# A gated cross-attention block with its slot order turned round: which projection follows the scores

## What the kernel computes

```
x      (8, 256, 128)   queries; ctx (8, 512, 128) keys and values; 16 heads of 64
xn     = layernorm(layernorm(x)) ;  q = xn @ w_q ;  k, v = split(ctx @ w_kv)
scores = einsum('bqhd,bkhd->bhqk', q * 64**-0.5, k) ;  attn = softmax(scores)
x      = x + tanh(g_xattn) * (attn @ v @ w_out + b_out) * tanh(gate)
tokens = layernorm(x) ; expert = argmax(softmax(tokens @ gate_w)), 8 experts, 160 places each
x      = x + tanh(g_ffn) * prob * (relu(token @ w1[expert]) @ w2[expert])
```

## Time and profile before

| | |
|---|---|
| device time, median of 3 runs | 523.41 us (522.75 to 524.91) |
| the profiled execution, its own time | 525.39 us |
| its span | 523.4 us |
| PE, DVE, ACT, POOL busy in the span | 82%, 74%, 65%, 70% |
| granted TensorE clock, mean over the span | 0.948 of full speed |
| DMA queue of SyncE, share of 16 engines | 82.9% |

### The profile page before, as it was taken

How to read it: one execution, slowest core, us unless ns; L and a number is a source line. 1 busy time by engine, 2 the same in 40 slices (tenths; PEclk the granted TensorE clock), 3 DMA queues, 4 the chain that set the end, 5 groups by cost and what they waited for, 6 DMA issues and landing times.

```text
span 523.4 us, 12954 instructions
## 1 busy us (share of the span) xinstructions
PE 430.0 (82%) x5084; PEld 347.4 (66%) x5084; DVE 389.0 (74%) x825; ACT 340.5 (65%) x548; POOL 365.2 (70%) x272
## 2 busy tenths in 40 slices
PE   5777886798899889988999889988988899663393
PEld 3455665677678767866777767776867687463393
DVE  4777888478997899888988898889888888703022
ACT  4575887267777877687768777777687767700140
POOL 2774768377797779777978697869876877741115
PEclk9797999699999999999999999999999999968598
DMA  7799999969999898989897989798979798970301
GB/s 220 220 168 174 176 207 232 201 123 173 182 155 189 148 173 177 171 148 173 178 190 139 163 176 203 120 183 157 183 138 173 154 175 142 182 123 11 102 11 40
DMA packets 285772, 83.13 MB, mean 159 GB/s; under 512 B 268404, under 2 KB 283172, under 8 KB 285713
## 3 DMA queue, kind: packets, MB, share of 16 engines
q1 hardware_dynamic: 284336, 79.01, 82.9%
q0 software_dynamic: 1376, 3.30, 1.8%
HBM read 10.83 MB, written 5.14 MB: 31 GB/s over the span
## 4 chain that ended last, share of the span: by engine, by line
PE 28%; POOL 21%; DVE 16%; issue 16%; ACT 11%; DMA 6%; SPq 1%; POOLq 0%; ACTq 0%; DVEq 0%
POOL PARTS L560 16%; DVE MXL L768 7%; ACT P L638 6%; PE psEF L963 5%; PE psX L1130 5%; DMA PT<-PARTS 4%; PE psAB L1038 3%; DVE HL L755 3%; PE psEF L965 3%; PE psEF L964 3%; DVE VL L761 2%; PE psCD L1038 2%; PE psEF L1229 1%; ACT VH L611 1%; ACT PARTS L648 1%
## 5 line engine op out<-in xcount | busy, mean ns | idle before, releaser
L560 POOL TENSOR_TENSOR PARTS<-P,PARTS 128x1024 f16<-128x1024 f32 x128 | 271.8, 2142 | 92.1 <-DVE PARTS L779 74.9
L1060 PE MATMUL psO<-VH,PT 128*128 128x65 f16 x1024 | 102.4, 195 | 15.8 <-DMA PT<-PARTS 15.8
L606 ACT ACTIVATE HL<-psEF 128x768 fp32r<-128x768 f32 x63 | 51.1, 812 | 85.7 <-PE psEF L965 85.7
L1060 PEld LDWEIGHTS psO<-VH,PT 128*128 128x128 f16 x1024 | 93.9, 98 | 18.3 <-DMA PT<-PARTS 10.8
L1061 PE MATMUL psO<-VL,PT 128*128 128x64 f16 x1024 | 102.4, 194 | 0.0
L1062 PE MATMUL psO<-VH,PT 128*128 128x65 f16 x1024 | 102.2, 195 | 0.0
L1061 PEld LDWEIGHTS psO<-VL,PT 128*128 128x128 f16 x1024 | 94.0, 99 | 0.6
L1062 PEld LDWEIGHTS psO<-VH,PT 128*128 128x128 f16 x1024 | 94.2, 98 | 0.0
L638 ACT ACTIVATE P<-psAB,NB 128x512 f32<-128x512 f32 x128 | 80.7, 687 | 5.5 <-DVE NB L771 5.5
L638 ACT ACTIVATE P<-psCD,NB 128x512 f32<-128x512 f32 x128 | 81.7, 701 | 0.2
L768 DVE TENSOR_REDUCE MXL<-psAB 128x2 f32<-128x1024 f32 x64 | 77.8, 1215 | 1.1 <-PE psAB L1038 1.1
(11 more groups left out here) (177 smaller groups left out, 762.3 us busy)
## 6 DMA issues: line engine op xcount, KB each, us to landing
ctx_raw<-in_ctx_dram SPq DMA_DIRECT2D x8, 256.0 KB, 3.7
w1s<-in_L_ffn_w_dram SPq DMA_DIRECT2D x8, 256.0 KB, 3.5
PT<-PARTS SPq DMA_TRANSPOSE x128, 4.7
w2s<-in_L_ffn_w_dram SPq DMA_DIRECT2D x8, 256.0 KB, 4.6
experts_table<-zeros POOLq DMA_DIRECT2D x2, 645.0 KB, 4.2
PARTS<-experts_table SPq DMA_DIRECT2D x2, 516.0 KB, 4.3
wraw<-in_L_xattn_w_kv_dram SPq DMA_DIRECT2D x4, 256.0 KB, 5.0
out_dram<-row SPq DMA_DIRECT2D x8, 128.0 KB, 2.8
```

The costliest lines, as they stand in the source:

```text
L560: pool.tensor_tensor(PARTS[:, par, qt, 1], P32[:, par, qt], PARTS[:, par, qt, 0], ALU.subtract).then_inc(plo_done, 1)
L606: act.activation(HL[:, hp % 2, H_KHI:H_KHI + KQ], kq_bank(j)[:, 0:KQ], ACT.Copy).then_inc(kq_hi_done, 1)
L1060: pe.matmul(psO[:, g:g + DH + 1], phi, VH[:, kt, head, 0:DH + 1], start=first_, stop=False)
```

## The change

The order of each engine's calls in a slot is turned round. No instruction is added or removed, and none changes its shape.

- TensorE: `v_project` (and `x_transposes`, `logits`) come directly behind the scores, then `values`, then `k_project` and `q_project`, then the transposes and `project`. The bank of V now has to be free of pair j+1, not of pair j+2.
- VectorE: `kq_lo` moves from behind the second maximum to the head of the next slot; `v_lo` (and `choose`) stand between the first and the second maximum. In slot hp = 3 `phi_first` and the normalising come ahead of `add_attention`.
- ScalarE: `v_hi` and `xt_hi` come ahead of the exponentials, `kq_hi` behind them; then `phi_second`, and the copies `ot_copy`, `ctxt_hi`, `tokt_copy` last.

```diff
 # ScalarE, batch(b)
                 for j, hp in slots(b):
+                    if v_group(b, hp):
+                        v_hi(*v_group(b, hp))
+                    if hp == X_STEP and not is_last(b):
+                        xt_hi(b + 1)
+                    exps(b, hp, 0)
+                    exps(b, hp, 1)
                     if not (is_last(b) and hp + AHEAD >= PAIRS):
                         kq_hi(*next_pair(b, hp, AHEAD))
-                    exps(b, hp, 0)
-                    exps(b, hp, 1)
+                    phi_second(b, hp)
                     if ot_group(b, hp):
                         ot_copy(*ot_group(b, hp))
                     if hp == CTX_STEP and not is_last(b):
                         ctxt_hi(b + 1)
...
-                    if v_group(b, hp):
-                        v_hi(*v_group(b, hp))
-                    phi_second(b, hp)
-                    if hp == X_STEP and not is_last(b):
-                        xt_hi(b + 1)
 # VectorE, batch(b)
                 for j, hp in slots(b):
+                    if j and not (is_last(b) and hp + AHEAD > PAIRS):
+                        kq_lo(*next_pair(b, hp, AHEAD - 1))
                     row_max(b, hp, 0)
+                    if v_group(b, hp):
+                        v_lo(*v_group(b, hp))
+                    if hp == LOGITS_STEP and not is_first(b):
+                        choose(b - 1)
                     row_max(b, hp, 1)
-                    if not (is_last(b) and hp + AHEAD >= PAIRS):
-                        kq_lo(*next_pair(b, hp, AHEAD))
+                    if j >= VALUES_BEHIND:
+                        normalise_heads(*back(b, hp, VALUES_BEHIND))
+                    phi_first(b, hp)
                     if hp == PROJECT_STEP and not is_first(b):
-                        phi_first(b, hp)
                         add_attention(b - 1)
                         token_moments(b - 1)
...
-                    if v_group(b, hp):
-                        v_lo(*v_group(b, hp))
-                    if hp == LOGITS_STEP and not is_first(b):
-                        choose(b - 1)
 # TensorE, batch(b)
                     scores(b, hp, 0)
                     scores(b, hp, 1)
+                    behind = min(j + AHEAD - 1, B * PAIRS - 1)
+                    if is_first(b) and hp == 2:
+                        pe.wait_ge(w_lo_rest_done, 3)
+                    if v_group(b, hp):
+                        v_project(*v_group(b, hp), behind=behind)
+                    if hp == X_STEP and not is_last(b):
+                        x_transposes(b + 1, behind)
+                    if hp == LOGITS_STEP and not is_first(b):
+                        logits(b - 1, behind)
+                    if j >= VALUES_BEHIND:
+                        values(*back(b, hp, VALUES_BEHIND))
                     if ahead:
-                        if is_first(b) and hp == 2:
-                            pe.wait_ge(w_lo_rest_done, 3)
                         k_project(*next_pair(b, hp, AHEAD))
                         q_project(*next_pair(b, hp, AHEAD))
...
-                    if j >= VALUES_BEHIND:
-                        values(*back(b, hp, VALUES_BEHIND))
-                    if v_group(b, hp):
-                        v_project(*v_group(b, hp), behind=j + AHEAD)
```

More of the change, by code:

```diff
@@ L891, in batch @@
                 for j, hp in slots(b):
+                    if j and not (is_last(b) and hp + AHEAD > PAIRS):
+                        kq_lo(*next_pair(b, hp, AHEAD - 1))
                     row_max(b, hp, 0)
+                    if v_group(b, hp):
+                        v_lo(*v_group(b, hp))
+                    if hp == LOGITS_STEP and not is_first(b):
+                        choose(b - 1)
                     row_max(b, hp, 1)
-                    if not (is_last(b) and hp + AHEAD >= PAIRS):
-                        kq_lo(*next_pair(b, hp, AHEAD))
+                    if j >= VALUES_BEHIND:
+                        normalise_heads(*back(b, hp, VALUES_BEHIND))
+                    phi_first(b, hp)
                     if hp == PROJECT_STEP and not is_first(b):
-                        phi_first(b, hp)
                         add_attention(b - 1)
                         token_moments(b - 1)
-                        normalise_heads(*back(b, hp, VALUES_BEHIND))
-                    else:
-                        if j >= VALUES_BEHIND:
-                            normalise_heads(*back(b, hp, VALUES_BEHIND))
-                        phi_first(b, hp)
                     if hp == X_STATS_STEP and not is_last(b):
@@ L986, in k_project @@
                 j = b * PAIRS + hp
-                if j == AHEAD:
-                    pe.wait_ge(kq_lo_done, 1)
-                elif j > AHEAD:
+                if j >= AHEAD:
                     pe.wait_ge(kq_lo_done, j)
```

## The result

The changed kernel takes **559.2 us** (median of 4 runs, 557.3 to 561.04) against 523.08 (4 runs); the ratio is 1.068, with a 95% interval of 1.064 to 1.073. It is slower by 36 us; 560 were forecast. The profiled execution took 557.3 us, with a span of 555.3.

A forecast was written before the change was run, and what follows sets the result against it. Bound before: VectorE's in-order queue plus V's round trip through TensorE and ScalarE. Profiled 525.39 + 29.7 + 0.7 + 2.5 + 4 = 562.3, less 1.98: median 560.3 us, 7% slower, range 545 to 571.

The forecast's parts named there:

- The loop of an ordinary slot: Closed loop kq_lo, V, second maximum, exponentials, kq_hi, kq_lo: 6.68 us a slot against 6.03 before.
- Slots 1, 3, 6 and 7: Slots with extra work: 8.80 us (context), 9.96 (output projection), 7.44 (choose) and 6.71 (place).
- The sum over batches 2 to 7: First maximum of batch 2 to that of slot 63: 345.9 us against 316.2, +29.7.
- Batches 0 and 1: Start of the kernel: 122.5 us against 120.1, +2.5, with ends of -1 and +6.
- the 3.7 us for the bias and the lower clock in batch 0: Batch 0 scales the bias behind phi_first and runs partly at the lower clock: about +3.7 us, estimated.
- the 3.5 us for the stall: VectorE's stall while w2's loads hold up slot 8's transposes: 3.5 us taken, between 0 and 7.08.
- The end: Short slot 62 lets slot 63 meet its values some 0.7 us before they can be ready: +0.7.
- The clock: TensorE idle 2.9 us behind slot 1, seven times, may lose full clock: 0 to 10.5 us, +4 taken.
- the second (fuller slots unchanged): Rival: context copy and projection slip into waits, so only the plain loop costs: 543 us, 9%.
- the third (late transposes): Rival: the transposed P lands late, values hold up kq_hi, up to 0.1 us a slot: 566 us, 5%.
- the fourth: Rival: faster; kq_hi is ready in time and the slot falls to VectorE's own 5.27 us: 491 us, 4%.
- The first (a fall in every batch, 1.5 us each): Rival: the clock falls in every batch and reaches keys and queries, 10.5 us in place of 4: 567 us, 15%.

The follow-up runs named there:

- Runs 1 to 4: Changed kernel, kq_hi between the exponentials: 561.9 us; kernel before, only kq_hi moved behind both exponentials: 618.1 us; then run 3 and run 4.
- Run 5: Changed kernel with ctxt_lo moved from the end of slot 1 to slot 2, between first maximum and v_lo: 545.2 us.
- run 6: Changed kernel with TensorE's output projection of slot 3 directly behind values, ahead of keys and queries: 555.2 us.
- Run 7: Changed kernel with the eight loads of w2 issued one a slot in slots 8 to 15, not all in slot 8: 555.6 us.
- the best kernel: Kernel before with choose and place ahead of v_lo, w2's loads spread, and V's high part ahead of ScalarE's ot_copy and tokt_copy: 506.1 us.
- run 4: Changed kernel with a copy of 512 columns added to each VectorE slot, ahead of the second maximum: 584.6 us.
- run 3: Changed kernel with a copy of 512 columns added to each VectorE slot, behind phi_first and add_attention: 566.6 us.

## Why the prediction was right, and where its sizes were off

- **The loop of an ordinary slot: right.** 6.68 forecast, 6.68 and 6.69 measured, with waits of 0.36 ahead of `v_lo` and 0.89 ahead of `kq_lo`. Counted start to start as in the forecast (0.08 more than from the recorded ends) these are 0.44 and 0.97, for 0.45 and 0.96. Runs 1 to 4 show that it is this loop and not VectorE's load. The weakest claim was that slots would be 6.23 with V's wait gone: no run tested it.
- **Slots 1, 3, 6 and 7: right** within 0.15 us. Run 5 shows slot 1's cause, run 6 slot 3's. The least exact is slot 3 (9.96 against 9.81): keys and queries started at 3.46 in the slot and not at 3.57, since they waited less for the copy of x than assumed, and `add_attention` and the moments held VectorE 1.44 us and not 1.50. Slot 0 was 0.09 longer than forecast.
- **The sum over batches 2 to 7: +29.7 forecast, +30.4 measured** (136.52 to 452.7 in the earlier trace rows, 138.13 to 484.66 after, 316.2 and 346.5 us). About 1.1 us of the 30.4 are falls of the clock, which the forecast has as a term of its own; without them it is 29.3. What is left are the small differences of slots 0, 1 and 3 in the table.
- **Batches 0 and 1: +2.5 forecast, +2.1 measured** (120.1 to 122.2), **which is luck.** The recorded terms add up to 2.4 and not to 2.5. They put batch 0 at 59.3 us and batch 1 at 63.1; they took 56.95 and 65.27. So the 3.7 us for the bias and the lower clock in batch 0 were too many by about 2.3, the 3.5 us for the stall too few by about 2.2, and the two errors cancelled. Slot 10 was 12.0 us, 5.3 more than an ordinary slot. The stall fell from the 7.08 of the earlier trace rows to 4.04 us at the division, with another 1.68 ahead of `kq_lo` right behind it:

```profile
96.18 0.18 DVE L786 RECIPROCAL rden<-psO 128x4 f32<-128x4 f32 x1 [4.04 <-PE psO L1056]
...
99.10 0.96 DVE L755 TENSOR_TENSOR HL<-psEF,HL 128x768 fp32r<-128x768 f32 x1 [1.68 <-ACT HL L606]
```

- **The end: +0.7 forecast, none measured.** The wait itself came: in slot 63 VectorE stood 1.70 us for the values of pair 61 (at 489.09), against 0.81 before, 0.9 more. The step that failed is that it reaches the end. From slot 63's maximum to the last division of the attention are 19.4 us before and 19.5 after, and to the end of the span 70.7 and 70.6, so the work in between took the wait back. Which part of it did so was not traced.
- **The clock: the mechanism right, the size too large for this execution.** TensorE's idle stretch ahead of V's projection at the end of slot 1 was forecast at 2.9 us and measured 2.75. Of the five full batches 2 to 6 of the changed kernel, three show a slot 2 of 7.0 us and two of 6.69. Windows over both kinds (length, busy of PE, PEld, DVE, ACT, POOL, then granted clock, DMA share, GB/s):

```profile
211.00:213.00 2.00, 0.00 (x0) 0.00 (x0) 0.95 (x2) 1.02 (x2) 2.00 (x2) 1.00 0.76 142
213.00:215.00 2.00, 1.34 (x21) 1.03 (x22) 1.90 (x3) 0.34 (x1) 1.99 (x3) 1.00 1.01 193
...
271.00:273.00 2.00, 0.00 (x0) 0.00 (x0) 1.43 (x2) 0.54 (x2) 2.00 (x2) 1.00 0.87 168
273.00:275.00 2.00, 1.82 (x19) 1.37 (x20) 1.43 (x4) 0.64 (x2) 1.99 (x3) 0.71 1.11 209
```

The same idle stretch (no matmul in the 2 us) is followed once by full clock and once by a fall to 1.2 GHz (granted clock 0.50 from 275.0 to 276.5). Each fall cost 0.32 in slot 2 and 0.06 in slot 3, together 1.1 us and not 4. But run 6, which does the same in slots 1 and 2, has one slot 2 of 8.13 us, with V and then keys at the lower level (granted clock 0.50 from 212 to 216): 1.44 over 6.69, the upper end that the prediction gave.

```profile
211.68 0.80 PE L960 MATMUL psEF<-w_hi,cT_hi 128*128 128x512 f32 x1 [2.76 <-DVE HL L755]
...
215.79 0.78 PE L960 MATMUL psEF<-cT_hi,w_hi 128*128 128x512 f32 x1
```

Run 7 has one of 8.10. In runs 6 and 7 the clock fell in four of the five batches, and their slots 2 lost 2.8 and 2.7 us together.

So the rule of the Trainium skill (TensorE: Matmul & The Clock Gate, "HAM oscillation — how this bites in real kernels"), that idling between bursts can cost the clock in each round, holds here as a risk that falls out differently each time, and not as a charge on every batch.

The profiled executions differ by 557.3 - 525.39 = 31.9 us, and the terms other than the clock and the end give that: 29.7 + 2.5 = 32.2 forecast, 30.4 + 2.1 - 0.5 (a shorter prologue) = 32.0 measured, where the 30.4 hold the 1.1 us of the clock. The medians differ by 36.1, which is nearer to the forecast's 36.9 than its terms deserve: that the median came out within 1.1 us of 560.3 is partly luck. The profiled execution before lies 2.3 above its median and that of after 1.9 below. How often the clock falls in an execution is a likely source of the latter. The four executions after took 557.3, 558.2, 560.2 and 561.0 us at mean granted clocks of 0.943, 0.946, 0.934 and 0.937: the two slower ones had the lower clock. With four executions, and no view of where the clock fell in three of them, this points that way and does not settle it.

Of the rivals, the second (fuller slots unchanged) is refuted by slots 1 and 3, the third (late transposes) appears only behind w2's loads and in slot 63, and the fourth is refuted by the 0.89 us ahead of `kq_lo`. The first (a fall in every batch, 1.5 us each) is refuted as a rule by the two batches without a fall; single slots of runs 6 and 7 paid that price.

## What to carry to other kernels

In a software-pipelined loop with in-order queues, look for the closed ring of handoffs and add it up, rather than for the busiest engine: the ring here predicted each slot of a full batch within 0.15 us where the clock did not fall, while the engines were idle for 20 to 38% of the span. Before moving a step from "early, with slack" to "late, cheap", follow its result to the next engine: `kq_hi` behind the exponentials cost 94 us alone. A wait that is already there is the best place for work that nobody needs soon (`choose`, `place`, the context's low part), and shortening the ring itself by one reordering on ScalarE gave the best kernel, 3.2% under the one before.

## What the runs showed of the hardware that was not expected

The added copy, from SBUF to SBUF on VectorE, takes 0.41 to 0.42 us when GpSimd computes nothing beside it. In slot 1 of run 4 it took 1.20 us. VectorE's copy, then GpSimd's two subtractions, in slot 1 and in the ordinary slot 5:

```profile
215.53 1.20 DVE L903 COPY fill<-fill 128x512 f32<-128x512 f32 x1
...
250.02 0.46 DVE L903 COPY fill<-fill 128x512 f32<-128x512 f32 x1
```

```profile
212.19 4.24 POOL L562 TENSOR_TENSOR PARTS<-P,PARTS 128x1024 f16<-128x1024 f32 x2
...
245.96 4.24 POOL L562 TENSOR_TENSOR PARTS<-P,PARTS 128x1024 f16<-128x1024 f32 x2 [2.83 <-DVE PARTS L781]
```

In slot 1 the subtractions end at 216.43 and the copy at 216.73; in slot 5 they end at 250.20 and the copy at 250.48. In runs 3 and 4, 51 copies start while a GpSimd computation still has at least 0.14 us to go. Of these, 49 end 0.27 to 0.30 us after it, however long it still ran. The other two stand beside rows in which the trace shows two GpSimd instructions as one. The order decides: the copies of run 3 that start about 0.16 us before a subtraction take 0.42 us, and the two subtractions that start during them take about 4.35 in place of 4.24. So a copy that finds GpSimd computing waits for the running instruction to end, and this wait shows as a longer copy and not as idle time. What the two engines share, the traces do not say.

This explains run 4. In batches 2 to 7 slot 1 grew by 1.10 to 1.21 us; in batches 0 and 1, where the copy took 0.42, it grew by 0.33. Over the 0.34 of the expectation that is 4.8 us. In most other slots the copy starts 0.15 to 0.26 us before GpSimd's end and holds VectorE 0.02 to 0.12 us longer than the 0.34. The clock fell in slot 2 too, which took 7.7 or 8.2 us in four of the batches 3 to 7.
